# The last batch's second norm between 24 and 8 of the previous batch's scatters, and the counting behind them

## The reference

```python
logits = x.astype(jnp.float32) @ router_w.T
probs = jax.nn.softmax(logits, axis=-1)
topk_w, topk_ids = jax.lax.top_k(probs, K)          # K = 8 of E = 64
...
pos = jnp.cumsum(onehot, axis=0)[jnp.arange(N), flat_e] - 1
valid = pos < C                                      # C = 128 slots per expert
idx = jnp.where(valid, flat_e * C + pos, E * C)
x_buf = jnp.zeros((E * C + 1, x.shape[1]), x.dtype).at[idx].set(x[tok])
...
contrib = y[safe] * (flat_w * valid.astype(flat_w.dtype))[:, None]
routed = jax.ops.segment_sum(contrib, tok, num_segments=T)
```

## Time and profile before

| | us |
|---|---|
| median of 3 runs | 2807.13 |
| lowest and highest run | 2803.64, 2812.64 |
| the profiled execution's own time | 2811.8 |
| its span, first to last instruction | 2810.1 |

### The profile page before, as it was taken

The page is one execution under the profiler, slowest core; times in us unless marked ns, Lnnn a source line. Parts: engine busy times, 40 slices in busy tenths (PEclk is TensorE's granted clock), DMA queues, the critical chain, the costliest instruction groups (busy, mean ns, idle before and its releaser), DMA issues. The chain is left out here.

```text
span 2810.1 us, 31463 instructions
## 1 busy us (share of the span) xinstructions
PE 2339.5 (83%) x10169; PEld 1174.3 (42%) x10169; DVE 1902.4 (68%) x3134; ACT 1673.5 (60%) x2352; POOL 1862.9 (66%) x1858
## 2 busy tenths in 40 slices
PE   5667777787777777775888799999999999999985
PEld 2222323232323323233555455555555555555543
DVE  5787989898988988763333356565756666666655
ACT  1778888889788888980122255555555555555440
POOL 0555587787878787873577302958585858595866
PEclk8667787878778787786899899999999999999997
DMA  3000000000000010114799500000000000000000
GB/s 104 16 1 1 17 16 16 18 16 18 9 25 8 10 23 3 30 15 107 218 265 226 112 1 1 1 1 23 1 23 1 23 1 20 4 8 1 9 0 16
DMA packets 94052, 98.97 MB, mean 35 GB/s; under 512 B 18848, under 2 KB 90656, under 8 KB 93856
## 3 DMA queue, kind: packets, MB, share of 16 engines
q1 hardware_dynamic: 70704, 73.99, 9.1%
q0 software_dynamic: 23152, 22.68, 4.6%
HBM read 69.98 MB, written 26.66 MB: 34 GB/s over the span
## 5 line engine op out<-in xcount | busy, mean ns | idle before, releaser
L1049 POOL TENSOR_TENSOR TT<-TT,SS 128x512 f32<-128x512 f32 x512 | 652.0, 1309 | 223.8 <-ACT SS L978 223.3
L1791 ACT ACTIVATE PR<-S,NM 128x512 f32<-128x512 f32 x512 | 345.3, 686 | 260.2 <-DVE NM L1958 260.2
L1958 DVE TENSOR_REDUCE NM<-S 128x2 f32<-128x1024 f32 x256 | 301.7, 1220 | 131.7 <-PE S L1685 131.7
L734 DVE TENSOR_SCALAR TT<-SC 128x1024 f32<-128x1024 f32 x256 | 311.6, 1217 | 75.4 <-POOL TT L1049 44.6
L464 PE MATMUL OB<-TT,VAL 128*17 128x512 f32 x1024 | 345.3, 777 | 4.6 <-ACT TT L986 4.6
L736 DVE SCALAR_TENSOR_TENSOR SS<-SC,TT 128x1024 f32<-128x1024 f32 x256 | 313.6, 1225 | 20.6 <-issue 1.8
L1054 POOL DMA_INDIRECT slot_tokens<-TID,IDX x224 | 229.3, 1024 | 101.1 <-issue 67.1
L1696 PE MATMUL TP<-ident,PR 128*128 128x128 f32 x2048 | 273.3, 276 | 21.2 <-DVE TT L1963 18.2
L1696 PEld LDWEIGHTS TP<-ident,PR 128*128 128x128 f32 x2048 | 235.0, 142 | 113.7 <-issue 66.9
L1963 DVE COPY TT<-TP 128x512 f32<-128x512 f32 x256 | 176.3, 689 | 151.4 <-PE TP L1696 147.6
L1797 ACT ACTIVATE TT<-TP 128x512 f32<-128x512 f32 x256 | 153.3, 599 | 195.1 <-PE TP L1696 191.3
(11 more groups left out here) (293 smaller groups left out, 4083.9 us busy)
## 6 DMA issues: line engine op xcount, KB each, us to landing
TT<-w_gu SPq DMA_DIRECT2D x64, 384.0 KB
TT<-w_dn SPq DMA_DIRECT2D x64, 128.0 KB
XL<-x SPq DMA_DIRECT2D x8, 512.0 KB
stream<-V SPq DMA_DIRECT2D x4, 1024.0 KB, 10.3
rows<-XL SPq DMA_DIRECT2D x8, 512.0 KB
TT<-w_dn SPq DMA_DIRECT2D x64, 64.0 KB
XS<-stream SPq DMA_DIRECT2D x8, 512.0 KB, 4.3
out<-XS SPq DMA_DIRECT2D x8, 512.0 KB, 2.9
```

The lines of the kernel that those rows point to most:

```text
L734: dve.tensor_scalar(tt[:, :, mt, :], SC[mt % 2][:], 0.0, None, ALU.max)
L1049: ins = pool.tensor_tensor(tt, tt, ss, ALU.add)
L1791: act.activation(PR[s % 2][h2][:], S[s % 2][:, h2, :], ACT.Exp, bias=NM[:, s % 2, h2:h2 + 1], accum_out=SM[:, pair % 2, j, h2:h2 + 1]).the ...
L1958: dve.tensor_reduce(NM[:, s % 2, :], S[s % 2][:], AX, ALU.max, negate=True).then_inc(sems["peak"], 1)
```

## The change

The two iotas with their drain and `counted` move from the head of POOL's last round to its end. Of batch 6's 32 scatters, 24 stay at `p` = 0 (`AHEAD` = 6 * SCATTERS = 24) and 8 move behind the power for `var2`, which is called at `p` = 4. Nothing else differs; DVE, PE, ACT and SP have the same instructions in the same order with the same waits.

```diff
+AHEAD = 6 * SCATTERS
...
                 if p == 4 and before:
                     rsqrt(v, 1, "var2", "rstd2")
-                if p == 0 and b == B:
+                if p == 4 and b == B:
+                    for c0 in range(AHEAD, NT * K, SCATTERS):
+                        scatter_of(v, c0)
                     pool.iota(count_i, [[1, P]], base=0, channel_multiplier=0)
                     pool.iota(own.bitcast(I32), [[0, 1]], base=0, channel_multiplier=1)
                     pool.drain()
                     pool.sem_inc(sems["counted"], 1)
                 if p == 0 and b == B:
-                    for c0 in range(0, NT * K, SCATTERS):
+                    for c0 in range(0, AHEAD, SCATTERS):
                         scatter_of(v, c0)
```

## The result

| us | before | changed |
|---|---|---|
| median | 2806.78 (20 runs) | 2801.25 (20 runs) |
| lowest and highest | 2800.73, 2812.64 | 2796.23, 2808.05 |
| the profiled execution's span | 2810.1 | 2799.1 |

The ratio is 0.9978, 95% interval 0.9972 to 0.9984: 5.5 us faster, where 17.0 were forecast. It lies within the 0.3% that the prediction called no change, and 0.25 us outside its range. The two profiled spans differ by more, 11.0 us: that of the kernel before came from an execution 4.7 us above the median of the first three.

What follows compares the result with a forecast made beforehand. The norm waited for POOL's power, late behind a drain and 32 scatters. Gains of 7.7 (drain) and 10.2 (eight scatters) less 0.9 (variance later) gave 17.0 us, other terms 0: 2807.1 - 17.0 = 2790.1 us, range 2784 to 2801.

Steps and rivals of the forecast that it cites:

- The iotas and the drain leave the head: POOL's last round in stage one: first scatter starts right behind the adds, 1245.2 instead of 1252.88, 7.7 us sooner.
- 24 scatters ahead: Ahead of POOL's power: they end at 1275.5, so the power starts at about 1276.4 instead of 1293.40, gain 17.0 us.
- The variance itself: DVE's last variance stays at 1276.33: taken as 0, with 0.9 us more gain or 7.15 us lost possible.
- Eight scatters behind the power: On POOL they run from 1277.7 to 1287.6; the table's load at about 1294.9 stays hidden, cost 0.
- The iotas and the drain at the end: POOL's `counted` comes at 1294.8 to 1295.5, 2.7 to 3.4 us before DVE's mark 0 asks: cost 0.
- rival 3: `counted` is late by a few us at DVE's mark 0: gain 13.5 us, time 2793.6, chance 0.09.
- PE's clock: PE idles to about 1279.0 instead of 1295.99 before the turned norm: taken as 0, 3 us either side.
- SP's queue: Table and weight loads go out 1294.9 to 1309.6, the stream's store due at 1322.2: 12.6 us cover, cost 0.
- Rivals 1 and 2: The standstill moves to stage two's first gather (chance 0.07) or stays ahead of the scatters (0.08): gain 10.2 us, time 2796.9.

Runs made afterwards that it cites:

- s3_none_ahead: Changed kernel with the power first, all 32 scatters, iotas and drain behind it; ratio 1.0039 to the kernel before.
- t1_eight_ahead: Changed kernel with iotas in the round before, no drain, 8 scatters ahead of the power and 24 behind; 2801.57 us, ratio 0.9989 to the kernel before.
- t2_sixteen_ahead: Changed kernel with iotas in the round before, no drain, 16 scatters ahead of the power and 16 behind; 2798.83 us, ratio 0.9972 to the kernel before.
- second set: Four variants of the changed kernel run on one chip: none ahead, iotas a round earlier, weights later, no drain with 16 ahead; kernel before 2801.52 us.
- e2_count_last: Changed kernel with all 32 scatters ahead of the power, iotas and drain behind it; 2804.19 us, ratio 0.9991 to the kernel before.
- s4_no_weights: Changed kernel with no expert's weights requested ahead of the table's load, all twelve behind it; ratio 1.0002 to the kernel before.
- e7_no_weights: Changed kernel with no expert's weights requested ahead of the table's load, all twelve behind it; 2793.44 us, ratio 0.9974 to the kernel before.

## Why the prediction was wrong

- *The iotas and the drain leave the head*, *24 scatters ahead*: right. The first scatter is 0.14 us behind the adds, the 24th ends at 1275.3.
- ***The variance itself* is the step that failed.** It says "the loads are the same and the scatters only start sooner, so I take 0". The row that spoke against it was named beside it, the 7.15 us "remote" of the earlier trace rows, and read as a constant. It was the same lateness that the later runs show, in its mildest form. Where signals were late, the first late one left PE some 13 to 18 us after the first scatter of the batch (9 to 10 us in the rows begun behind the power, in s3_none_ahead, t1_eight_ahead and t2_sixteen_ahead). Before, the row began at 1252.88 and the turned attention output passed 7.6 and 8.9 us later, on time; only the second output product was caught. With the row 7.6 us sooner the turned output at 1260 is caught, and two signals in turn come 11.3 and 6.0 us late. The term was sized at 0 with 7.15 us at worst; it measured 12 us (38.05 - 32.9 = 5.1 us gained instead of 17.0). That the sooner row does it is shown by the variance moving with the number ahead; that it does so in every execution is not, because of the second set.
- *Eight scatters behind the power*: 1289.95 for the first is the late variance again. What the step lacked is the pause of 5.40 us ahead of the last scatter.
- *The iotas and the drain at the end*, cost 0: also wrong, by 4 to 5 us. The tail of 7.50 us was right in size (7.0 behind the iotas, 7.4 behind the last scatter). The reading that a drain ends some 7 us behind whatever work stands in front of it was not: in e2_count_last it ends 0.5 us behind the iotas. The cover of 2.7 us was eaten by the pause ahead of the last scatter (5.40 where 0.30 is usual) and by the clock, which brought DVE 3.4 us sooner: 2.7 - 5.1 + 0.5 for the shorter tail - 3.4 = -5.3, and DVE waits 5.78. This is rival 3 in its place, by other causes.
- *PE's clock*, 0 within 3 us: it gave 3.4 us. The hole was gone ahead of the norm, so PE came to it busy (9.76 of the 10 us from 1280 on, and the granted clock rose there) and not from 24.65 us idle.
- *SP's queue*: the table's load goes out at 1312.19 and the PW store at 1326.91, with the stream's store at 1336.47 behind them. It still costs nothing that the table shows, but without the drain and with shorter rows it is the table that DVE waits for next.
- *Rivals 1 and 2*: the first gather still starts 0.9 us behind the stage's start, and the first scatter 0.14 us behind the adds. By the Trainium skill's rule (GPSIMD Engine Reference, Instruction dispatch) freshly loaded code pays about 6 us at its first call. No run here shows that pause, and none tests it for `iota`: the set-up calls iotas at 4.58 us of e2_count_last already, and the drain behind those at 1297.12 ends 0.5 us after them. A pause did move, though, to a place that no rival named: ahead of the last of the 32 scatters.

Why the signals are late is open. Three things are not told apart: whether PE's signal travels late, whether PE itself finishes later than the profile's modelled ends say, or whether the recording holds them up. And what made the four profiles of one set free of it wasn't found; the kernel before itself was 5 us faster there, and their traces hold some 3,000 more semaphore updates.

## What to carry to other kernels

A wait that a profile puts down to "remote" or "issue" is not a constant of the instruction it stands at. Before something is moved, ask what was in flight when it occurred and how long ago that had begun, and price the case that it catches the chain's signals. Suspect long unbroken rows of indirect DMAs beside stretches in which engines hand small pieces to each other; shorter rows brought the variance forward here, but not the time. Don't put a drain on POOL behind them: let the last writers count the semaphore themselves. The best version outside the second set does that: the changed kernel without its drain, ratio 0.9955 and 0.9959 in two sets. And see whether two profiles recorded the same things before comparing their waits.

## What the runs showed of the hardware that was not expected

- Beside a row of 16 or more indirect scatters from POOL (one every 1.26 us) single signals of PE to ACT and DVE were taken 5 to 20 us behind PE's recorded end, in all 16 profiles outside the second set (in s3_none_ahead only behind the logits, where a copy of the shared expert waited 18.5 us and it cost nothing, since DVE then still waited 7.85 us for the counts), and in none of the four inside it. They came as late with a DMA share of 0.02 to 0.03 (s4_no_weights), and on time with 253 GB/s and no scatter (s3_none_ahead). The 16 profiles with late signals are also those with semaphore updates missing.
- A POOL drain behind scatters ended 6.5 to 8.6 us behind the last scatter's recorded end in all 20 profiles, whatever stood between them. The Trainium skill, Perfetto Trace Analysis, section DMA Instruction — SWDGE (GPSIMD), says that the recorded end is that of descriptor generation and not of the data's movement. That agrees, if the drain waits for the movement, which the median of 7.8 us from issue to landing of the last 32 scatters in e7_no_weights also suggests. The drain at the head in the earlier trace rows had no scatter within 27 us in front of it and ended 6.78 us behind the last iota all the same; that stays unexplained.
- The last of the 32 scatters starts after a pause of 4.4 to 6.8 us in all 16 profiles without a drain at the head of the round, and after 0.30 us in the four with one, whatever was ahead of it. Where this pause comes from wasn't tried.
